# Four layers in one kernel: x loads, gates and the second and third triangular solutions in a new order

## The reference

```
x = LN(x + delta_rule_attention(x))   # 4 heads of 32, chunks of 32 tokens
x = LN(x + moe(x))                    # 8 experts, hidden 256, top 2, all experts computed
x = LN(x + linear_recurrence(x))      # block-diagonal gates, scan over the tokens
x = LN(x + ternary_ffn(x))            # 128 -> 512 -> 512 -> 512 -> 128
```

```
A = -(beta*k @ k.T) * strictly_lower
T = inverse of a unit triangular 32x32 system made from A   # fori_loop of 31 row updates
u, w = T @ (beta*v), T @ (beta*k)
per chunk in order:  u' = u - w @ S;  o = q @ S + causal(q @ k.T) @ u';  S = S + k.T @ u'
```

## Time and profile before

| what | value |
|---|---|
| median of 3 runs | 866.82 us (866.6 to 869.07) |
| the profiled execution, its own time | 869.17 us |
| its span, first to last instruction | 867.3 us |
| mean granted TensorE clock | 0.958 |
| TensorE busy | 806.4 us, 93% |
| VectorE busy | 615.7 us, 71% |
| ScalarE busy | 486.7 us, 56% |
| GpSimd busy | 485.3 us, 56% |

### The profile page before, as it was taken

The page is one execution under the profiler, slowest core; times in us unless marked ns, Lnnn a source line. Parts: engine busy times, 40 slices in busy tenths (PEclk is TensorE's granted clock), DMA queues, the critical chain, the costliest instruction groups (busy, mean ns, idle before and its releaser), DMA issues.

```text
span 867.3 us, 11901 instructions
## 1 busy us (share of the span) xinstructions
PE 806.4 (93%) x3812; PEld 626.2 (72%) x3812; DVE 615.7 (71%) x1162; ACT 486.7 (56%) x766; POOL 485.3 (56%) x507
## 2 busy tenths in 40 slices
PE   4999798889878999899989999999999999999997
PEld 3777686777557777777777678777877787776775
DVE  2666977787679658776866687668776876777553
ACT  3878345333753474358435664585457546757754
POOL 0049698767546637973786355435553454357342
PEclk9999798588979999999989999999999999999999
DMA  3124436300320020003000400030020000000000
GB/s 133 49 78 119 116 116 171 110 25 0 86 61 26 10 77 1 1 11 88 1 1 2 122 0 2 11 86 0 0 71 26 0 0 1 13 0 1 13 12 13
DMA packets 37903, 35.81 MB, mean 41 GB/s; under 512 B 1632, under 2 KB 30816, under 8 KB 37856
## 3 DMA queue, kind: packets, MB, share of 16 engines
q1 hardware_dynamic: 37856, 35.22, 14.5%
HBM read 21.85 MB, written 13.37 MB: 41 GB/s over the span
## 4 chain that ended last, share of the span: by engine, by line
PE 56%; POOL 14%; issue 8%; DVE 7%; ACT 2%; DVEq 0%; ACTq 0%; POOLq 0%
PE bank L439 56%; POOL tpm L1242 4%; POOL tmp L1239 4%; POOL fbl L1298 2%; POOL acc L1306 2%; DVE spread L1538 2%; DVE sexp L1554 1%; DVE fbh L1750 1%; DVE yg L1564 1%; POOL texp L1268 1%; DVE fbl L1748 1%; ACT fbh L1090 1%; DVE fah L1807 0%; DVE ttp L1434 0%; POOL fal L1337 0%
## 5 line engine op out<-in xcount | busy, mean ns | idle before, releaser
L1084 ACT ACTIVATE hf<-bank 128x512 f32<-128x512 f32 x64 | 38.3, 598 | 176.9 <-PE bank L439 171.3
L1298 POOL TENSOR_TENSOR fbl<-hf,fbh 128x512 fp32r<-128x512 f32 x64 | 81.9, 1280 | 74.4 <-DVE fbh L1750 74.4
L1239 POOL TENSOR_TENSOR tmp<-apm,tpm 128x31 f32<-128x31 f32 (+15 forms) x124 | 78.3, 631 | 51.2 <-DVE apm L1425 43.9
L439 PEld LDWEIGHTS bank<-pk,spread 128*128 128x128 f32 x640 | 83.7, 209 | 19.4 <-DVE spread L1538 13.4
L439 PE MATMUL bank<-pk,spread 128*128 128x64 f32 x640 | 86.5, 294 | 8.1 <-DVE spread L1538 7.3
L1329 POOL TENSOR_TENSOR fbl<-hf,fbh 128x512 fp32r<-128x512 f32 x28 | 36.9, 1319 | 89.9 <-DVE fbh L1807 89.9
L1242 POOL TENSOR_TENSOR tpm<-tpm,tmp 128x31 f32<-128x31 f32 (+15 forms) x124 | 79.9, 644 | 9.7
L1306 POOL TENSOR_TENSOR acc<-acc,yg 128x512 f32<-128x512 f32 x48 | 64.6, 1346 | 35.7 <-DVE yg L1564 35.7
L1748 DVE TENSOR_TENSOR fbl<-hf,fbh 128x512 fp32r<-128x512 f32 x64 | 59.6, 931 | 32.1 <-ACT fbh L1090 30.8
L1564 DVE TENSOR_TENSOR yg<-bank,gb 128x512 f32<-128x512 f32 x64 | 43.9, 685 | 36.2 <-PE bank L439 36.1
L439 PE MATMUL bank<-fal,wfh 128*128 128x512 f32 x160 | 67.6, 423 | 0.0
(11 more groups left out here) (240 smaller groups left out, 2231.9 us busy)
## 6 DMA issues: line engine op xcount, KB each, us to landing
pk<-pack SPq DMA_DIRECT2D x7, 1280.0 KB, 7.1
pack<-pk SPq DMA_DIRECT2D x5, 1280.0 KB, 6.7
ws<-in_wf SPq DMA_DIRECT2D x11, 256.0 KB, 2.9
pack<-pk SPq DMA_DIRECT2D x4, 640.0 KB, 4.1
xs<-in_xh SPq DMA_DIRECT2D x8, 262.0 KB, 5.6
xt<-in_xh SPq DMA_DIRECT2D x8, 262.0 KB, 3.0
ws<-in_wm SPq DMA_DIRECT2D x8, 256.0 KB, 2.7
tt<-ttp SPq DMA_DIRECT2D x4, 512.0 KB, 3.1
```

What stands on the lines that cost most here:

```text
L439: return P.matmul(out, lhsT, rhs, start=start, stop=stop, skip_group_check=skip)
L1084: A.activation(hf[:, 0, :], bank[4][:, :], ACT.Gelu).then_inc(S["gelu_done"], 1)
L1239: G.tensor_tensor(m, a, r, ALU.mult).then_inc(S["t_mul"], 1)
L1298: G.tensor_tensor(fbl[:, sl, :], hf[:, 1, :], f32(fbh[:, sh, :]), ALU.subtract)\
```

## The change

- SyncE, lead: the x of tile t + 3 is loaded ahead of iteration t's weight pieces and pack store, where before it was the x of tile t + 2 (tile 2's load keeps its place).
- TensorE, lead: at tile 1 the projection of tile 2's q comes behind the gram products of tile 1.
- VectorE, lead: at tile 4 `solve_out(0)` comes ahead of the two `gram_rows`, not behind them.
- ramp2: on VectorE, `gate_weights` and `gate_rows` come ahead of `value_rows` and `gram_rows(6, 0)`; on TensorE, `gate_turn` ahead of `gram(6, 1)`. SyncE stores solution 1 behind pieces 15 and 16 and tile 6's pack.
- The weighting is cut out of `solve_out` as `solve_weight`. Solutions 0 and 3 do both as before. Solution 1 is weighted in dense(0) at expert 1; solution 2 is turned at expert 4 and weighted at expert 5 of dense(1), where before both stood at expert 2, ahead of `solve_in(3)`, which stays there.

```diff
@@ SyncE, lead
             load_xs(1)
+            load_xs(2)
             for t in range(LEAD - 1):
-                load_xs(t + 2)
+                if t < LEAD - 2:
+                    load_xs(t + 3)
                 for p in PIECES[t][2:] + PIECES[t + 1][:2]:
                     load_piece(p)
                 if t:
@@ SyncE, ramp2
                 load_next(a + 1)
-                store_tt(1)
                 for p in PIECES[s][2:] + PIECES[s + 1][:1]:
                     load_piece(p)
                 store_pack(s)
+                store_tt(1)
                 load_piece(PIECES[s + 1][1])
@@ TensorE, lead
                     project(t + 1, 0)
-                    project(t + 1, 1)
                     if t != 1:
+                        project(t + 1, 1)
                         project(t + 1, 2)
...
                 if t == 1:
+                    project(t + 1, 1)
                     project(t + 1, 2)
@@ TensorE, ramp2
                 up(a, 0)
+                gate_turn(a)
                 gram(s, 1)
-                gate_turn(a)
@@ VectorE, solve_out
                 dve.wait_ge(S["t_turned"], p + 1)
+                if p not in (1, 2):
+                    solve_weight(p)
+
+            def solve_weight(p):
+
+                ttp = ttps[p // 3]
                 tt(ttp[:, :, :], ttp[:, :, :],
@@ VectorE, lead
+                if t == LEAD - 1:
+                    solve_out(0)
                 gram_rows(t, 0)
                 gram_rows(t, 1)
...
-            solve_out(0)
             split_pieces(PIECES[LEAD - 1][:2])
@@ VectorE, ramp2
                 top_two(a)
+                gate_weights(a)
+                gate_rows(a)
                 value_rows(s)
                 gram_rows(s, 0)
-                gate_weights(a)
-                gate_rows(a)
                 gram_rows(s, 1)
@@ VectorE, dense
                 for e in range(E):
+                    if isinstance(m, int) and m == 0 and e == 1:
+                        solve_weight(1)
...
                     if inv == 1 and e == 2:
+                        solve_in(3)
+                    if inv == 1 and e == 4:
                         solve_out(2)
-                        solve_in(3)
+                    if inv == 1 and e == 5:
+                        solve_weight(2)
```

## The result

| kernel | runs | median us | from, to | ratio to before (95%) |
|---|---|---|---|---|
| before | 20 | 866.04 | 861.91, 869.48 | |
| changed | 20 | 860.06 | 856.13, 864.95 | 0.9937 (0.992 to 0.9954) |

The median is 6.0 us lower. Forecast were 859.9 and 6.9 us less. A run over 1.5% above the fastest of its kernel is left out of a ratio; in all that follows it is one, half_first's 868.33. The profiled execution of the changed kernel took 859.76 us (span 857.9, mean granted clock 0.968); that of before took 869.17 (867.3, 0.958), so the two profiles stand 9.4 us apart, more than the medians do. Nor can their absolute times be compared as they are: the changed profile is ahead by 1.2 us at VectorE's copy of `s3row`, 22.16 us into the span instead of 23.37, which nothing edited precedes.

A forecast was written before the change was run, and what follows sets the result against it. Bound by TensorE (56% of the chain) and GpSimd (14%), GpSimd alone from 108 to 152 us; 4.6 + 0.8 + 1.5 = 6.9 us takes the median 866.82 to 859.9, range 855.5 to 864.

The forecast's parts named there:

- Waits for x: Lead: VectorE's waits of 4.99 and 4.69 us for tiles 4 and 5 go; TensorE's 3.67 shrinks to 0.5 to 1.
- `solve_out(0)`: Lead, VectorE: reached at 95.9 without waiting, solution 0 ended at 94.7; TensorE then idles 5 us before `beta(5)`.
- ramp1: Stretch after `solve_out(0)`: `delta_spread(0, 0)` 3.0 us earlier, only 0.7 usable at half clock; gain taken as 1.9.
- `attention_sum`: ramp2, VectorE: starts at 150.0 to 152.3 instead of 155.77, 3.5 to 5.8 us earlier, taken 4.6; weighting 1.48 of it.
- Gates first: ramp2 into dense(0): new gate order, less a store wait of 1.6 to 2.5, gains 0.1 to 1.6 us, taken 0.8.
- Weighting at expert 1: Dense(0), VectorE: solution 1's weighting costs 1.23 to 1.48 us; by the skill's rule it could delay GpSimd by 1.23.
- Dense(1): Turn and weighting of solution 2 leave expert 2, where TensorE idled 2.5 us: 0 to 2.5 won, taken 1.5.
- The sum: Whole kernel: 4.6 + 0.8 + 1.5 = 6.9 us faster; 9.9 at the good end, 3.6 at the bad.
- the clock stays full: Rival: idle times shrink, the 5 us before `beta(5)` do not lower the clock, all good ends come true: 856.9; chance 0.16.
- The clock eats the ramp: Rival: half clock from 100 to 109 us and in the gates, nothing from dense(1): 3.6 won, 863.2; chance 0.17.
- Slower: Rival: idle before `beta(5)` brings half clock lasting beyond 125 us, `attention_sum` 5 us late: 870; chance 0.06.
- three signs of being wrong: `solve_out(0)` waits for GpSimd; half clock over 10 us after 100 us; gain by 170 us not there at 310.

The follow-up runs named there:

- half_first: Changed kernel with `value_rows` and `gram_rows(6, 0)` on VectorE between `gate_weights` and `gate_rows`; 857.30 us, ratio to before 0.9901.
- x_only: Kernel before with only SyncE's lead edit, the x loads a tile ahead; 860.84 us, ratio to before 0.9944.
- after_again: The changed kernel run once more, unedited, for a second profile; 860.41 us, ratio to before 0.9936.
- gates_old: Changed kernel with the gate order of before on VectorE and TensorE; 859.95 us, ratio to before 0.9941.
- before_again: The kernel before run once more, unchanged, for a second profile; 863.18 us, ratio to before 0.9985.
- rest_only: Kernel before with all edits but the lead's (gates first, both weightings moved, store moved); 867.34 us, ratio to before 1.0018.
- lead_w1: Kernel before with the lead's edits and solution 1's weighting at expert 1, old gate order, solution 2 at expert 2; 861.24 us, ratio to before 0.9954.
- sol2_old: Changed kernel with solution 2's turn and weighting back at expert 2 of dense(1), ahead of `solve_in(3)`; 860.95 us, ratio to before 0.9957.
- pad_tails: Changed kernel with 9 needless TensorE matmuls ahead of tile 0's first feed-forward product after dense(1); 862.31 us, ratio to before 0.9966.
- gram4_first: Changed kernel with `solve_out(0)` behind `gram_rows(4)` again, as before; 864.59 us, ratio to before 0.9988.
- half_again: The half_first kernel once more, in another set beside the changed kernel; 853.90 us, ratio to before 0.9892.
- lead_only: Kernel before with only the lead's edits on SyncE, TensorE and VectorE; 864.36 us, ratio to before 0.9984.

## Why the prediction was right, point by point

*Waits for x.* Right. Both are gone, the gram of tile 4 waits 0.80 us (0.5 to 1 forecast), and x_only shows the loads alone to bring 2.9 of the 4.8 us.

*`solve_out(0)`.* Right: no wait, the turn at 94.39 plus the start's 1.2 us makes 95.6 on the time axis of before, where 95.9 stood; solution 0 ended at 94.06 + 1.2 = 95.3, where 94.7 stood. The 5 us of idle TensorE before `beta(5)` came as 5.05.

*ramp1, 0.7 to 3.0, taken 1.9.* Right in its mechanism, the upper end a little low. The range is that of TensorE's use of `delta_spread(0, 0)`, which comes behind the chunk and twelve matmuls: 3.3 us earlier here, 2.5 in after_again, 1.6 in gates_old, where half clock lasted 3.4, 6.8 and 10.2 us. VectorE's own instruction came 4.9 earlier, not 3.0. The step took the pieces between at their old 5.0 us. They took 3.45 (98.81 to 102.54, less 0.28 of waiting), because VectorE's cast ran in 0.70 where it took 2.38 beside GpSimd before.

*`attention_sum`, 3.5 to 5.8, taken 4.6.* The range lies between two kinds of execution rather than around one: 7.0 in the first profile, 3.6 in after_again. Two paths end at the turn, GpSimd's last row and VectorE's `beta_rows(6)` behind ScalarE and TensorE. The prediction had the second come last, and that is after_again: the turn there, on the time axis of before, is at 150.15, in its 148.0 to 150.3. In the first profile GpSimd's row came last, by 1.03 us, as it did in before, and it came 5.6 us earlier, not 4.5. So TensorE's speed does not matter here in the kernel before (before_again), and in the changed kernel it does. The weighting's part is 1.5 in rest_only, as forecast.

*Gates first, 0.1 to 1.6, taken 0.8.* Right in its parts, wrong in what it is owed to. The distance to `delta_spread(1, 0)` was 11.0 (10.3 at full clock, 12.8 at half; after_again has 13.1) and the wait for the store 2.32 (1.6 to 2.5). But the old order needs 10.18 in gates_old and is as fast, rest_only's new order at half clock needs 12.95 where before needed 12.62, and lead_w1 against sol2_old has the new order 1.8 us behind at expert 1. The 0.8 was no gain of the order: the step compared it at full clock with the old order at half.

*Weighting at expert 1.* I took 1.23 to 1.48. It took 2.13 in the changed kernel, sol2_old and pad_tails, 2.11 in lead_w1, 1.44 to 1.63 in gates_old, gram4_first, half_first, rest_only and after_again, and 1.25 in half_again. The Trainium skill (SBUF — State Buffer, SBUF: two separate sides) says that of a VectorE instruction with two SBUF inputs and a GpSimd instruction that reads SBUF the one that starts first holds their shared port for its whole length, and the other waits. The trace agrees. In the changed kernel GpSimd's low part had begun at 163.21, 0.23 us before the weighting, and kept its 1.28; the weighting ended 1.08 after it (165.57 and 164.49). GpSimd's multiply behind it took 1.57 where before had 0.59 (at 171.84). In half_again the weighting began first, at 161.04, and kept 1.25, and GpSimd's low part took 2.26:

```profile
163.21 1.28 POOL L1301 TENSOR_TENSOR fbl<-hf,fbh 128x512 fp32r<-128x512 f32 x1 [2.43 <-DVE fbh L1765]
164.44 1.57 POOL L1242 TENSOR_TENSOR tmp<-apm,tpm 128x231 f32<-128x231 f32 x1
...
161.17 2.26 POOL L1301 TENSOR_TENSOR fbl<-hf,fbh 128x512 fp32r<-128x512 f32 x1
```

The prediction took the 0.25 us between the earlier trace rows to show less than the rule. But that weighting, at 154.37 in before, met a GpSimd operation that had only 0.40 us left (it ended at 154.77), and it too ended 1.08 after it.

*Dense(1), 0 to 2.5, taken 1.5.* 2.0 in the profiles; 1.57 of it is TensorE's waits of 1.34 and 1.14 shrinking to none and 0.91. In the medians sol2_old shows 0.9 that can't be told from nothing.

*The sum* of 6.9 met 6.0, and some of that is luck. At like clock the change is worth 3.4 and 4.4 us in the two outer groups, near the sum's bad end of 3.6, and 6.0 only between them. That more of its runs were at the higher clock is no term of the sum.

Of its rivals, *the clock stays full* did not come, although `attention_sum` passed its good end: full clock held after the 0.80 us before tile 4's gram, but half clock came in the 5.05, after the 1.30 and after the 1.11. *The clock eats the ramp* is what after_again's profile shows up to the gates, with dense(1)'s 2.0 us kept all the same, and its execution took 866.25, above that rival's 863.2. So forecast and rival were not two outcomes of the kernel but two kinds of its executions, and the median lies between. *Slower* failed by its own point of decision: half clock at the idle 5 us lasted 3.4 us, or 6.8 (after_again), or 10.2 (gates_old), and was over by 107.

Of the three signs of being wrong one came: granted clock after 100 us was at half for over 10 us at a time, 129.8 to 140.0 and 153.7 to 174.2 in after_again. The other two did not: `solve_out(0)` does not wait, and what is won by 170 us is there at 310. That it would be kept to the end holds within what the clock does: 1.5 us are lost behind dense(1) in the changed kernel's first profile, and the two profiles of before differ by 3.0 there.

What stays open: why the lower clock came in 7 of 12 runs of lead_only, 11 of rest_only and 8 of gram4_first, but in 1 of x_only's and after_again's and none of the 9 of gates_old. With 9 to 12 runs each that may be the kernels' or chance; no single place was found that decides it. Nor is the mean clock independent of the kernel, so the table by clock is evidence and no proof.

## What to carry to other kernels

Follow one gain through anchors that are counted from the first instruction that no edit precedes, in two profiles of each kernel, before a difference is put down to an edit: here the two profiles of before differ by 3.7 us by the end of dense(1), and those of the changed kernel by 4.8. Part the runs by their granted clock as well, or an edit of 0.2 to 0.5% is lost in how many of them fell in which group. Where a small load stands behind a large store in the one queue, moving it ahead of the store is a cheap edit, and alone it had nearly the whole gain of the medians here (x_only, 0.9944). And where a step is brought forward past the rows that release a store, look at who waits for the store: putting those rows in the gap that the step itself has (half_first, half_again) came with another 2.8 and 6.5 us in the medians, of which the profiles put 2.6 at this place.

## What the runs showed of the hardware

- Within one kernel the time goes with the mean granted clock. The outer groups of the table above lie 6.7 us apart in before and 5.7 in the changed kernel, as much as the change is worth.
- Half clock (1.2 GHz) came after idle times as short as 1.20 us (before, 131.91), and in other executions idle times of 1.19 (before_again, 131.10) and 1.31 (lead_w1 and sol2_old, at 128.3) left the clock full. Nor did its length follow from that of the idle time: it lasted 3.4, 6.8 or 10.2 us with the 5.05 us of idle before `beta(5)`, and 3.4 or 10.2 after 1.3.
- VectorE's operations stretch beside GpSimd, and GpSimd's beside VectorE: the same weighting took 1.22 to 2.13 us, GpSimd's low part 1.28 or 2.26. Of the two, the one that began first kept its time. The cast of 128x512, with one input, took 0.42, 1.43 or 2.38. The cast of 1.43 (at 148.30) stood, but for its first 0.25 us, beside two memsets of GpSimd, which read nothing.
